# Attention scores of two units as 32-row products side by side, issued behind the value products

## The reference, cut to what matters

```python
x = x + 0.5 * ffn(layernorm(x))
x = x + attention(layernorm(x))        # 16 heads of 16 channels, windows of 128 tokens, stride 64
x = x + 0.5 * ffn(layernorm(x))

# attention, for every batch, head and window n (tokens 64n .. 64n+127)
scores = q_win @ k_win.T * 0.25 + pos_bias[head]
out[window] += softmax(scores) @ v_win      # then divided by how often a token is covered, then @ Wo + bo
```

## Time and profile before

| | us |
|---|---|
| median of 3 runs | 1555.97 |
| lowest and highest run | 1555.27, 1557.31 |
| span of the profiled execution | 1558.5 |
| PE busy in it | 1341.3 (86%) |
| DVE busy | 924.5 (59%) |
| ACT busy | 645.8 (41%) |
| POOL busy | 246.7 (16%) |

### The profile page before, as it was taken

How to read it: one execution, slowest core, us unless ns; L and a number is a source line. 1 busy time by engine, 2 the same in 40 slices (tenths; PEclk the granted TensorE clock), 3 DMA queues, 4 the chain that set the end, 5 groups by cost and what they waited for, 6 DMA issues and landing times.

```text
span 1558.5 us, 32504 instructions
## 1 busy us (share of the span) xinstructions
PE 1341.3 (86%) x8323; PEld 858.5 (55%) x8324; DVE 924.5 (59%) x3760; ACT 645.8 (41%) x2323; POOL 246.7 (16%) x279
## 2 busy tenths in 40 slices
PE   4412799999996899989899999989994699999996
PEld 4411466666664456656566565656653366666664
DVE  5789444444443567787687877787784244444442
ACT  1114322232222476656566665656661132222221
POOL 4323001000102101021111112020212101100100
PEclk9999999999998899999999999999996799999998
DMA  9500442000002101020201111020206221000000
GB/s 301 206 28 31 171 151 58 13 13 13 17 13 88 48 21 42 22 56 21 57 9 38 33 32 46 21 56 21 56 9 242 59 58 55 17 13 13 13 17 14
DMA packets 57278, 85.55 MB, mean 55 GB/s; under 512 B 8848, under 2 KB 40848, under 8 KB 57168
## 3 DMA queue, kind: packets, MB, share of 16 engines
q1 hardware_dynamic: 50352, 65.49, 13.7%
q0 software_dynamic: 6816, 18.81, 3.4%
HBM read 45.81 MB, written 27.97 MB: 47 GB/s over the span
## 4 chain that ended last, share of the span: by engine, by line
PE 66%; DVE 12%; issue 6%; ACT 2%; POOL 2%; DMA 1%; SPq 1%; another core or an unknown queue 1%; DVEq 0%; ACTq 0%; POOLq 0%
PE bank L797 24%; PE bank L926 9%; PE bank L749 9%; PE bank L815 9%; PE bank L952 6%; PE bank L886 4%; DVE w_all L1364 3%; DVE w_all L1373 2%; PE bank L912 2%; DVE hb L1210 2%; PE bank L963 2%; ACT sl L629 2%; PE bank L763 1%; PE bank L899 1%; POOL sorted_rows L504 1%
## 5 line engine op out<-in xcount | busy, mean ns | idle before, releaser
L709 ACT ACTIVATE w_all<-w_all 128x128 f32<-128x128 f32 x896 | 349.7, 393 | 223.1 <-DVE w_all L1364 222.0
L797 PE MATMUL bank<-w_all,xt 128*128 x1680 | 391.2, 383 | 11.5 <-DVE xt L1222 3.5
L1364 DVE CUSTOM_DVE_ANT_0 w_all<-bank,w_all 128x128 f32<-128x128 f32 x896 | 207.3, 287 | 133.8 <-PE bank L926 123.5
L797 PEld LDWEIGHTS bank<-w_all,xt 128*128 128x128 f16 x1680 | 165.3, 98 | 196.7 <-issue 37.3
L1210 DVE SCALAR_TENSOR_TENSOR hb<-bank,ew,sl 128x512 f32<-128x512 f32 x140 | 105.1, 751 | 207.2 <-ACT sl L629 207.2
L815 PE MATMUL bank<-w_all,ht 128*128 x1680 | 206.2, 273 | 1.2 <-DVE yt L1235 1.2
L629 ACT ACTIVATE sl<-bank,back 128x512 f32<-128x512 f32 x140 | 95.9, 685 | 238.6 <-PE bank L797 221.8
L749 PEld LDWEIGHTS bank<-ident,w_all 128*128 128x128 f32 x896 | 112.6, 142 | 119.9 <-issue 113.2
L815 PEld LDWEIGHTS bank<-w_all,ht 128*128 128x128 f16 x1680 | 164.2, 98 | 19.4 <-issue 1.7
L709 ACT ACTIVATION_READ_ACCUMULATOR w_all<-w_all 128x1 f32 x896 | 169.8, 189 | 0.0
L1373 DVE COPY w_all<-bank 128x512 f32<-128x512 f32 x224 | 153.7, 686 | 1.3 <-PE bank L749 1.2
(11 more groups left out here) (163 smaller groups left out, 1585.5 us busy)
## 6 DMA issues: line engine op xcount, KB each, us to landing
big<-sorted_rows SPq DMA_DIRECT2D x70, 130.5 KB
saved<-w_all SPq DMA_DIRECT2D x16, 512.0 KB
w_all<-saved SPq DMA_DIRECT2D x4, 2048.0 KB, 14.2
w_all<-mid SPq DMA_DIRECT2D x9, 512.0 KB, 3.6
big<-in_L_attn_hidden_states SPq DMA_DIRECT2D x8, 512.0 KB, 4.2
w_all<-in_L_ffn_gate_w SPq DMA_DIRECT2D x8, 512.0 KB
w_all<-in_L_ffn_up_w SPq DMA_DIRECT2D x8, 512.0 KB
w_all<-in_L_ffn_down_w SPq DMA_DIRECT2D x8, 512.0 KB
```

The costliest lines, as they stand in the source:

```text
L709: a = nc.scalar.activation(prob[:, u % NB, h], sbias[:, u % NB, h], ACT.Exp, bias=nmax[:, u % NB, h:h + 1], scale=-1.0, accum_out=rsum[:, ...
L797: mm = nc.tensor.matmul(bank[2 * e + w][:], xt[:, hx, c, :], flat(gu16[:, bass.ds(g * E + e, 1), w, hw, c, :]), start=(i == 0), stop=(i == ...
L1364: i = nc.vector.tensor_tensor_reduce(out=sbias[:, u % NB, h], in0=bank[u % 2][:, h * W:(h + 1) * W], in1=nbias[:, (u % NQ) * HQ + h], scal ...
```

## The change

- Keys: ACT writes the projected keys twice, once multiplied by a mask that keeps the even heads' rows and once by one that keeps the odd ones (`kmask`, `kb`), straight into `km[par]`, which has two buffers. `kt`, the 16 mask DMAs of each batch, their semaphores and the zeroing of `km` go.
- Scores: the product of a unit becomes four products over 32 rows (two heads) with 256 columns for one pair of units: for each half `c` of the channels and each of the two units q0 and q0+1, rows `32q` to `32q+31`. The two units write two different banks. Two units are scored in one call, in even steps only, for u+2 and u+3, behind `values(u-1)` and ahead of `factors` and the side work.
- Heads: a unit now has heads 2q, 2q+1, 8+2q, 8+2q+1 (`head_at`). In `values` its four heads write four different groups of 32 partitions, and units q even and q odd add up in the same place (`slot_at`). The value and output weights are permuted to match: `Wv` and `bv` by eight POOL copies, `Wo` by loading it in eight pieces, which are issued later.
- Banks: unit u uses bank u%4 for its scores and then for its transposes. `turn` no longer waits for `pt_ready`, `scores` no longer for `sb_ready`.

```diff
-            def scores(b, par, u, early):
-                n, q = divmod(u, NQ)
+            def scores(b, par, u, freed):
+
+                n, q0 = divmod(u, NQ)
                 if u == 0:
-                    pe.wait_ge(km_loaded[0], (b + 1) * (16 * HC) + OPEN)
+                    pe.wait_ge(k_ready, (b + 1) * DC)
                     pe.wait_ge(q_ready, (b + 1) * DC)
-                if u == 3 * NQ:
-                    pe.wait_ge(km_loaded[1], (b + 1) * (16 * HC) + OPEN)
-
-                if not early:
-                    pe.wait_ge(sb_ready, b * UNITS + (u - 1))
-                nc.tensor.matmul(bank[u % 2][:].rearrange("p (h k) -> p h k", h=HQ),
-                                 qt[par][:, q * HQ // HC, n * STRIDE:n * STRIDE + W],
-                                 km[:, q * HQ:(q + 1) * HQ, n * STRIDE:n * STRIDE + W],
-                                 start=True, stop=True).then_inc(s_done, 1)
-
-            def turn(b, u, early):
+                if freed is not None:
+                    pe.wait_ge(pt_ready, freed)
+                win = slice(n * STRIDE, n * STRIDE + W)
+                for c in range(DC):
+                    for q in (q0, q0 + 1):
+                        rows = slice(q * HS, (q + 1) * HS)
+                        mm = nc.tensor.matmul(bank[q][:, c * 2 * W:(c + 1) * 2 * W].rearrange("p (e k) -> p e k", e=2),
+                                              qt[par][rows, c, win], km[par][rows, c, :, win], start=True, stop=True)
+                        if c == DC - 1:
+                            mm.then_inc(s_done, 1)
+
+            def turn(b, u):
                 pe.wait_ge(p_ready, b * UNITS + (u + 1))
-                if not early:
-                    pe.wait_ge(pt_ready, b * UNITS + (u - 1))
                 for h in range(HQ):
-                    tr = transpose(bank[2 + u % 2][:, h * W:(h + 1) * W], prob[:, u % NB, h])
+                    tr = transpose(bank[u % NQ][:, h * W:(h + 1) * W], prob[:, u % NB, h])
                 tr.then_inc(pt_psum, 1)
...
-                    m, pair = divmod((q * HQ + h) // 2, HC // 2)
-                    mm = nc.tensor.matmul(bank[4 + (par + n) % 2][HS * pair:HS * (pair + 1), m * W:(m + 1) * W],
-                                          va[par][:, n, q * HQ + h, :], pt_s[:, u % 2, h * W:(h + 1) * W],
-                                          start=(h % 2 == 0), stop=(h % 2 == 1))
+                    m = q // 2
+                    mm = nc.tensor.matmul(bank[4 + (par + n) % 2][HS * h:HS * (h + 1), m * W:(m + 1) * W],
+                                          va[par][:, n, slot_at(q, h), :], pt_s[:, u % 2, h * W:(h + 1) * W],
+                                          start=(q % 2 == 0), stop=(q % 2 == 1))
...
                 for u in range(UNITS):
-                    if ahead(b, u, last):
-                        b2, u2 = ahead(b, u, last)
-                        scores(b2, par if u2 > u else 1 - par, u2, False)
-                    turn(b, u, first_ and u < 2)
+                    turn(b, u)
                     if u:
                         values(b, par, u - 1, first_)
                     elif not first_:
                         values(b - 1, 1 - par, UNITS - 1, False)
+                    if u % 2 == 0 and ahead(b, u, last):
+                        b2, u2 = ahead(b, u, last)
+                        scores(b2, par if u2 > u else 1 - par, u2, None if first_ and u == 0 else b * UNITS + u)
...
-            def copy_k(b, m):
+            def copy_k(b, par, m):
                 act.wait_ge(proj_done, b * NPROJ + (m + 1))
-
-                if m == 0:
-                    act.wait_ge(km_loaded[1], b * (16 * HC) + OPEN)
-                nc.scalar.activation(kt[:, m, :], bank[6 + m][:], ACT.Identity, bias=qkb[:, 1, m:m + 1]).then_inc(k_ready, 1)
+                for e in range(2):
+                    a = nc.scalar.activation(km[par][:, m, e, :], bank[6 + m][:], ACT.Identity, bias=kb[:, e, m:m + 1],
+                                             scale=kmask[:, e:e + 1])
+                a.then_inc(k_ready, 1)
...
-            sp.dma_start(wo_s, Wo.rearrange("(c p) n -> p c n", p=P)).then_inc(aw_loaded, 16)
-            sp.dma_start(bo_s, bo.partition_broadcast(P)).then_inc(aw_loaded, 16)
...
-                    sp.wait_ge(k_ready, b * DC + 2 * DC)
-
-                    sp.wait_ge(s_done, b * UNITS + 4 * NQ + OPEN)
-                    mask_keys(b + 1, 0)
-
...
-                    sp.wait_ge(s_done, b * UNITS + UNITS + OPEN)
-                    mask_keys(b + 1, 1)
```

More of the change, by code:

```diff
@@ L58 @@
 NPROJ = 2 * DC + TB
-ATTN_LOADS = 9
+ATTN_LOADS = 7
+WO_LOADS = 9
+APADS = 2
+VPERM = 8
+MASK_STEPS = 4
 SHIFTS = 2
@@ L93, in macaron_kernel @@
         tiles_i = big[:, :].bitcast(I32).rearrange("p (t r) -> p t r", r=RW)
-        km = big[:, 0:H * S].rearrange("p (h s) -> p h s", h=H)
+        km = [big[:, k * 2 * DC * S:(k + 1) * 2 * DC * S].rearrange("p (c e s) -> p c e s", c=DC, e=2) for k in range(2)]
         ident = sb("ident", [P, P])
@@ L196, in macaron_kernel @@
         qkb = part(3, DC)
+        kmask = part(2)
+        kb = part(2, DC)
+        kbits = part(1)
         inv_count = part(NWIN)
@@ L314, in two_by_two, with head_at, slot_at @@
             batch(B - 1, 1, False, True)
+        def head_at(q, i):
+            return (i // 2) * HC + 2 * q + i % 2
+        def slot_at(q, i):
+            return (q // 2) * HC + 2 * i + q % 2
         def which(k):
@@ L410, in load_batch @@
                 sp.dma_start(xb, rows_of(b)).then_inc(xb_loaded, 16)
[L412 to L418, removed]
             def shift_values(b, par):
@@ L448, in _ @@
             load_batch(1)
[L450 to L453, removed]
+            load_wo()
+            sp.wait_ge(apads_made, APADS)
             shift_values(0, 0)
@@ L551, in _ @@
                 for half in range(2):
-                    pool.wait_ge(*((icount_made, 2 * n + half) if n or half else (apads_made, 3)))
+                    pool.wait_ge(*((icount_made, 2 * n + half) if n or half else (apads_made, APADS)))
                     pool.memset(inv_count[half * STRIDE:(half + 1) * STRIDE, n:n + 1],
@@ L557, in _ @@
             pool.wait_ge(aw_loaded, 16 * ATTN_LOADS)
+            wv_from = wv_in.rearrange("p (d c m l e i) -> p d c m e l i", d=DC, c=2, m=DC, l=2, e=2)
+            wv_to = wv_s.rearrange("p d (m c e l i) -> p d m c e l i", m=DC, c=2, e=2, l=2)
+            bv_from = bv_in.rearrange("p (c m l e i) -> p c m e l i", c=2, m=DC, l=2, e=2)
+            bv_to = bv_s.rearrange("p (m c e l i) -> p m c e l i", m=DC, c=2, e=2, l=2)
+            for m in range(DC):
+                for c in range(2):
+                    pool.tensor_copy(wv_to[:, :, m, c], wv_from[:, :, c, m]).then_inc(wv_ready, 1)
+                    pool.tensor_copy(bv_to[:, m, c], bv_from[:, c, m]).then_inc(wv_ready, 1)
+            pool.wait_ge(wo_loaded, 16 * WO_LOADS)
             def accumulate(b, par, n):
@@ L731, in _ @@
             copy_xnt(prep_use(0))
-            copy_k(0, 0)
-            copy_k(0, 1)
+            copy_k(0, 0, 0)
+            copy_k(0, 0, 1)
             copy_q(0, 0, 0)
@@ L1031, in _ @@
             pe.wait_ge(v_ready, TB)
-            scores(0, 0, 0, True)
-            scores(0, 0, 1, True)
+            scores(0, 0, 0, None)
             two_by_two(pe, batch)
@@ L1337, in _ @@
             dve.wait_ge(y_ready, NS + OPEN)
-            nc.vector.memset(km[:, 0:H // 2], 0.0).then_inc(km_zero, 1)
+            mask = Chain(mask_step, 0)
+            mask(nc.vector.tensor_single_scalar(kbits.bitcast(I32), token_no[:, 0:1], 4, ALU.arith_shift_right))
+            mask(nc.vector.tensor_single_scalar(kbits.bitcast(I32), kbits.bitcast(I32), 1, ALU.bitwise_and))
+            mask(nc.vector.tensor_copy(kmask[:, 1:2], kbits.bitcast(I32)))
+            mask(nc.vector.tensor_scalar(kmask[:, 0:1], kmask[:, 1:2], -1.0, 1.0, ALU.mult, ALU.add))
+            assert mask.n == MASK_STEPS
             dve.wait_ge(xb_loaded, 16)
@@ L1342, in _ @@
             dve.wait_ge(aw_loaded, 16 * ATTN_LOADS)
+            for e in range(2):
+                nc.vector.tensor_scalar(kb[:, e, :], qkb[:, 1, :], kmask[:, e:e + 1], None, ALU.mult).then_inc(kb_ready, 1)
             nc.vector.tensor_scalar(nbias[:], nbias[:], -1.0, None, ALU.mult).then_inc(nbias_ready, 1)
@@ L1362, in biased @@
                 for h in range(HQ):
-                    i = nc.vector.tensor_tensor_reduce(out=sbias[:, u % NB, h], in0=bank[u % 2][:, h * W:(h + 1) * W],
-                                                       in1=nbias[:, (u % NQ) * HQ + h], scale=1.0, scalar=BIG,
+                    i = nc.vector.tensor_tensor_reduce(out=sbias[:, u % NB, h], in0=bank[u % NQ][:, h * W:(h + 1) * W],
+                                                       in1=nbias[:, head_at(u % NQ, h)], scale=1.0, scalar=BIG,
                                                        op0=ALU.add, op1=ALU.min, accum_out=nmax[:, u % NB, h:h + 1])
```

31 lines of the change are left out of this document (19 added, 12 removed).

## The result

The kernel after takes 1637.08 us, median of 4 runs (1635.06 to 1646.12), against 1555.62 (1550.7 to 1557.31) for the kernel before in the same comparison: 1.0537 times as long, interval 1.0505 to 1.0569. The forecast was 1586, range 1548 to 1622. It is slower, as forecast, but by 81 us and not by 30.

The account below looks back on a forecast made before the run. PE's sum of work was taken to bound the kernel before, a PE-DVE-ACT loop the attention stage after. Chain 18, clock 13, start -0.5 gave +30 us on the 1558.5 span; median 1586, range 1548 to 1622.

Parts of the forecast that it names:

- the clock's: Attention stage: clock falls now and then to 1.2 GHz as PE waits; a tenth of the stage slow, 13 us taken.
- the rival: Clock falls often in attention: a quarter of the stage or more at half clock, 1605 to 1625 us; chance 0.15.
- The chain's sum: Attention: loop through PE, DVE and ACT replaces PE as bound; 2 us more a batch, some 18 over eight.
- The terms in a pair: Pair of attention steps without side work: two units' scores 1.07, transposes 0.59, values 0.38; pair 4.98 us, before 4.12.
- The wait of `values` in the pair: Attention pair without side work: PE waits 1.26 us before the value products, room that hides even steps' side work.
- the 79.9 us for a batch of before: Attention batch before the change, PE's work summed: steps 57.7 plus side work 22.2 us; the rows had 81.6.
- a forecast of 81.9: Attention batch after the change: 14 pairs, 69.7 us, plus 12.2 of side work sticking out of the waits.
- The start: Ahead of the first batch's input: two loads leave the queue, 0 to 1 us less, 0.5 taken.
- masks and key copies cost nothing: Key preparation: dropping 128 mask DMAs changes nothing; ACT's second key copy, about 0.6 us twice a batch, lies in idle time.
- the clock falls often: Rival in attention: a quarter of the stage or more at half clock, 18 + 38 us and more, 1605 to 1625; chance 0.15.
- The row products do run side by side: Two units' 32-row scores overlap, 1.07 us not 1.92; rival that they don't: 1615 to 1635 us, chance 0.08.
- How far side work fits into the waits: Rival in attention: only part of a batch's 12.2 us side work sticks out; at 7 us, 1530 us; chance 0.13.

Follow-up runs that it names:

- e8: Kernel after with the transposes of steps 1, 3, 5, 15 and 19 of a batch repeated, value products not repeated: 1607.06 us, ratio 1.0328.
- e9: Kernel before with scores reading only rows 0 to 31 of queries and masked keys, so output is not the layer's: 1661.46 us, ratio 1.0701.
- e6: Kernel after, but with 32-row scores of one unit at the start of each step, ahead of its transposes: 1645.68 us, ratio 1.0577.
- e5: Kernel before with 128-row scores of two units issued together behind the even step's values, banks by u%4: 1614.00 us, ratio 1.0376.
- e11: Kernel before with two units' 128-row scores issued late, behind the even step's values, and value products in four groups: 1589.92 us, ratio 1.0231.
- e7: Kernel after with scores ahead of the even step's values, plus repeated transposes and value products as useless PE work: 1553.98 us, ratio 0.9994.
- e10: Kernel before with scores reading only rows 0 to 63 of queries and masked keys, so output is not the layer's: 1624.72 us, ratio 1.0458.
- e1: Kernel after with some transposes and value products issued once or twice more, as useless work in PE's waits: 1584.68 us, ratio 1.0202.

## Why the forecast was wrong

**The step that failed** is the clock's: "If a tenth of the stage is slow, 60 us x 1.5/6.5 = 14 us; none is the one bound, a quarter (38 us) the other. I take 13." Slow are 271.7 of 718.8 us, 38%, above the upper bound too. The price in it was sound (1.5/6.5 = 0.23 against 0.24 and 0.27 measured, 0.21 and 0.35 by way of e8, a slow pair 6.59 us against 6.5); the share was not. (271.7 - 6.8) x 0.27 = 72 us stand where 13 stood. Behind the size lay a wrong cause: I took the share of time in which PE works as what the clock goes by, and the earlier trace rows bore only on that, where every product reads 128 rows. e9 and e6 show the clock at 0.50 with PE at work all the time, e5 shows it kept with PE waiting, and from e11 to after, where only the scores' form and what prepares it change, the slow time goes from 30.4 to 271.7 us. The Trainium skill (TensorE: Matmul & The Clock Gate, Part 1) ties the clock to how busy PE has been; the measurement goes against it in so far as busy time is what one reads in a profile. I also read a stretch of 1.91 busy us in 3.4 that kept the clock as an argument against the rival. It was a stretch of 128-row work.

**The chain's sum** was 18 us. What is left for it is an estimate, about +6 to +8 (644.5 against 638, and 78.8 less 72); with prices of 0.21 and 0.35 it would be +23 and -14, so no run shows that 18 was too much. The terms in a pair were right: products side by side, scores block 1.07, values 0.36 (0.38), pair 4.96. The wait of `values` in the pair shown is 0.72 and not 1.26 because the 0.55 us of `factors` lie in it, which is the cover that the working counted on. Too low was the 79.9 us for a batch of before, whose batches from the second on take 80.9 to 88.1: a forecast of 81.9 set against them is no loss.

**The start**: 0.5 us less forecast, 2.1 us less outside the stage measured. That masks and key copies cost nothing stands: none of PE's waits above names them.

**Sum**: +7 chain, +72 clock, -2 outside = +77, and the span has +76.7. The chain's 7 is what the clock's price leaves over, so that the sum closes proves neither.

**The rivals.** That the clock falls often was the right mechanism, given 0.15 and at most 1625: its price was bounded by a quarter of the stage, and the time lies above its range. The row products do run side by side. How far side work fits into the waits is not shown for the chain as it stands; e7, with the scores one place earlier and most of the clock kept, comes to 1553.98, not the 1530 of that rival.

**Still open** is what of a 32-row product the clock goes by. Its rows, graded by e9, e10 and before, are shown; whether the switch between shapes, which those two have and before has fewer of, plays a part in it is not, and was not tried; it does not explain the difference between e9 and e10, which have equally many. In e9 and e10 the heads that are left out get scores of zero, so the numbers that PE works on change as well; whether that matters was not tried either. How far PE's waits add to the rows' effect is shown only in so far as filling them helped (e1, e8).

## What to carry to other kernels

A bare pair read from latencies can be right to 0.02 us and the forecast still wrong, when the clock is a share guessed. Before products are cut to 32 rows, run the kernel before with 32 rows of its operands (e9): one run shows that the clock is at stake, though not how much (129.7 us slow there, 271.7 in the kernel after). And take a change apart: its values in four groups alone run at 1525.45 us, 1.9% less than before and 6.8% less than after, while the late place (+52 us) and the row form (+50 us) each cost more than that gives.

## What the runs showed that I had not expected

- With PE busy 34.00 of 34.00 us on work whose scores read 32 rows, the granted clock stays at 0.50; later the same work stands at 1.00 for 228.6 us. Fewer rows make the clock come back late: slow stretches of up to 44.4 us with 32 rows, 34.1 with 64, 3.4 with 128.
- With the 32-row products of one unit a step (e6) the clock fell while PE was busy without a break.
- 1408 more matmuls, all of them useless, make the kernel 52 us faster (e1), the transposes among them alone 30 us (e8).
- A slow microsecond costs 0.21 to 0.35 us where a loop over three engines sets the end, and about 0.44 where PE does.
- Products of fewer rows among 128-row ones cost some 0.18 us a step by estimate, although columns and count are the same (e9, e10).
